# Silu of a gate and of a convolution by ScalarE's own function over whole blocks, and a re-timed order, in a fused attention, Mamba and recurrent kernel

## The reference

```python
xz = einsum('btd,de->bte', x, in_proj_w)            # 256 -> 2 x 512
x_branch, z = split(xz, 2)
xb = depthwise_conv(x_branch, conv_w, 4 taps) + conv_b
x_branch = silu(xb)                                  # "xc" in the kernel
B_t, C_t, dt = split(x_branch @ x_proj_w, [16, 16, 1])
dt = softplus(dt * dt_proj_w + dt_proj_b)
h = exp(dt * A) * h + dt * B_t * x_branch            # 16 states, scan over time
y = (sum_s h * C_t + D * x_branch) * silu(z)
return y @ c_proj_w
```

## Time and profile before

| | |
|---|---|
| median of 3 runs | 1284.66 us (1284.48 to 1288.39) |
| the profiled execution, its own time | 1291.45 us |
| span of the profile within it | 1290.1 us |
| TensorE busy | 1144.3 us (89%) |
| VectorE busy | 1172.5 us (91%) |
| ScalarE busy | 781.7 us (61%) |
| GpSimd busy | 981.8 us (76%) |
| mean granted clock | 0.968 |

### The profile page before, as it was taken

One profiled execution on the slowest core, in us unless ns is written; L12 is line 12 of the kernel. 1 busy time (PEld: TensorE's weight loads), 2 busy tenths in 40 slices (PEclk: granted clock), 3 DMA queues, 4 the chain that ended last, 5 costly groups with the idle time before them and its releaser, 6 DMA issues.

```text
span 1290.1 us, 12503 instructions
## 1 busy us (share of the span) xinstructions
PE 1144.3 (89%) x3574; PEld 640.0 (50%) x3574; DVE 1172.5 (91%) x1161; ACT 781.7 (61%) x1447; POOL 981.8 (76%) x713
## 2 busy tenths in 40 slices
PE   6767967898899989998999899998999898789896
PEld 4533523474447543673447543673447443444454
DVE  3666899999999999999999999999999999999987
ACT  2226645856667657855767657865776666645532
POOL 3213795889879897989878997989878996976852
PEclk9778988999999999999999999999999999899999
DMA  6406567775768678876769687876868676899922
GB/s 252 139 5 220 209 226 258 282 261 213 250 227 303 235 251 290 288 259 224 251 227 308 213 281 277 299 251 212 265 219 302 219 270 219 303 322 345 371 88 98
DMA packets 92309, 313.87 MB, mean 243 GB/s; under 512 B 10432, under 2 KB 15680, under 8 KB 91984
## 3 DMA queue, kind: packets, MB, share of 16 engines
q1 hardware_dynamic: 89216, 303.77, 68.1%
q10 hardware_dynamic: 3024, 9.31, 2.0%
HBM read 301.73 MB, written 11.31 MB: 243 GB/s over the span
## 4 chain that ended last, share of the span: by engine, by line
PE 40%; DVE 28%; POOL 12%; issue 9%; ACT 6%; DMA 4%; DVEq 0%; SPq 0%; POOLq 0%; ACTq 0%
DVE ps L1667 15%; PE ps L857 14%; POOL arena L1894 6%; PE ps L568 5%; DVE ps L1390 4%; PE ps L791 4%; DVE arena L1673 3%; PE ps L576 3%; DMA arena<-bc_scratch 2%; PE ps L695 2%; PE ps L703 2%; PE ps L711 2%; PE ps L718 2%; PE ps L600 1%; DVE stats_before L1271 1%
## 5 line engine op out<-in xcount | busy, mean ns | idle before, releaser
L1894 POOL TENSOR_TENSOR arena<-arena 128x1024 f32<-128x1024 f32 x255 | 600.2, 2361 | 157.3 <-PE ps L857 126.1
L1667 DVE TENSOR_TENSOR_SCAN ps<-ps,arena 128x1024 f32<-128x1024 f32 (+1 forms) x257 | 585.8, 2280 | 24.6 <-ACT ps L1236 15.8
L857 PE MATMUL ps<-arena,identF 128*128 128x512 f32 x1024 | 485.4, 605 | 47.2 <-DVE arena L1673 28.3
L1236 ACT ACTIVATE ps<-arena,negA 128x512 f32<-128x512 f32 x512 | 333.0, 683 | 87.4 <-DVE arena L1673 82.5
L857 PEld LDWEIGHTS ps<-arena,identF 128*128 128x128 f32 x1024 | 190.9, 194 | 267.6 <-issue 203.0
L1673 DVE TENSOR_TENSOR arena<-ps,arena 128x1024 f32<-128x1024 f32 x256 | 311.8, 1218 | 5.7
L872 ACT ACTIVATE arena<-arena,rnln 128x256 f32<-128x256 f32 x120 | 63.0, 589 | 50.9 <-POOL rnln L1700 37.6
L614 PE MATMUL ps<-arena,inw 128*128 128x512 f32 x128 | 62.5, 635 | 20.0 <-ACT arena L881 9.6
L1390 DVE SCALAR_TENSOR_TENSOR ps<-arena,vecs,ps 128x512 f32<-128x512 f32 x96 | 64.8, 747 | 5.9 <-ACT ps L985 5.9
L695 PE MATMUL ps<-arena,inw 128*128 128x512 f32 x128 | 61.1, 600 | 3.3 <-DVE arena L1554 3.3
L881 ACT ACTIVATE arena<-ps,modT 128x512 f32<-128x512 f32 x45 | 54.1, 1267 | 13.9 <-PE ps L454 13.5
(11 more groups left out here) (220 smaller groups left out, 1675.9 us busy)
## 6 DMA issues: line engine op xcount, KB each, us to landing
arena<-bc_scratch SPq DMA_DIRECT2D x511, 512.0 KB, 5.0
arena<-in_x SPq DMA_DIRECT2D x16, 256.0 KB, 6.7
arena<-in_x SPq DMA_DIRECT2D x8, 512.0 KB, 8.1
xr_scratch<-arena SPq DMA_DIRECT2D x6, 512.0 KB, 6.6
px_scratch<-arena SPq DMA_DIRECT2D x6, 512.0 KB, 7.0
out_x<-arena SPq DMA_DIRECT2D x5, 512.0 KB, 2.6
arena<-bc_scratch SPq DMA_DIRECT2D x9, 256.0 KB, 3.6
rowmod<-mod_scratch SPq DMA_DIRECT2D x4, 512.0 KB, 8.7
```

Source lines behind the costliest of these rows:

```text
L857: x = pe.matmul(ps[:, Y, :], identF[:], inp[:, m % RING, q, :], start=False, stop=(i == BLOCK_STEPS - 1 and q == 1), skip_group_check=True)
L1236: x = act.activation(ps[:, 2 * (m % 2) + q, :], dt[:, kd, :], ACT.Exp, scale=negA[:, kd, 2 * i + q:2 * i + q + 1])
L1667: x = dve.tensor_tensor_scan(states, states, inp[:, m % RING, q, :].rearrange("p q t -> p (q t)"), 0.0, ALU.mult, ALU.add)
L1894: x = pool.tensor_tensor(inp[:, m % RING, :, :], u[:, kd:kd + 1, :].broadcast_to([P, 2, TH]), b_at[:, m % 3, :, :], ALU.mult)
```

## The change

Both silus are computed by ScalarE's `Silu` function over larger tiles in SBUF.

- z: ScalarE copies each kd from the bank to `sz` (four copies of 128x512), which frees the bank, and then computes Silu once over all of `sz`, 128x2048, in place. The first gate of a half waits for that one instruction. `dve_z` is gone.
- convolution: VectorE's third tap writes its sum to `xc` instead of the bank; ScalarE computes Silu in place over `xc` of kd 0 and 1 and of kd 2 and 3 (two of 128x1024), both behind the last tap. `dve_silu` and the tanh are gone. TensorE's channels of kd 2 and 3 now wait for the last tap of kd 0 and 1.
- Silu and Exp are in different tables of ScalarE, as are Softplus and Exp, so ACT_TABLE_LOAD instructions stand around each new Silu. The program has 49 of them, where it had 18.
- the factors 1/2 that were folded into D, `dtw`, the projection weights and `GA1` go, with four small instructions at the start.
- `TIMES` has new numbers nearly throughout, for all five engines.

```diff
-MAMBA = ["pad", "xb_mm", "xc_init", "conv", "xc_tanh", "xc", "z_mm", "z_tanh", "z_ev", "bc_mm", "bc_sb", "softplus", "spare",
+MAMBA = ["pad", "xb_mm", "xc_init", "conv", "xc", "z_mm", "z_ev", "z_silu", "bc_mm", "bc_sb", "softplus", "spare",
...
-    "pe_after": {"c_proj": (1, 3.75), "z": (5.25, 6, 7.25, 9), "hnA_t0": 10.25, "hnA_t1": 11,
+    "pe_after": {"c_proj": (1, 3), "hnA_t0": 8.75, "hnA_t1": 9.25, "gate_x": (11.25, 12.75, 17, 17.75, 20.75, 23.75),
+        "gate_c": (11.25, 12.75, 17, 17.75, 20.75, 24.75), "px": (25, 26), "om": 26, "z": (4, 5, 6, 6.75)},
...
                 if kd >= 2:
-                    pe.wait_ge(S.xc, 4 * h + kd - 1)
+                    pe.wait_ge(S.conv, conv_done(h, kd - 2, TAPS - 2))
...
+        def act_silu(h, p):
+
+            act.wait_ge(S.conv, conv_done(h, 2 * p + 1, TAPS - 2))
+            act.activation(xc_pair(h, p), xc_pair(h, p), ACT.Silu).then_inc(S.xc, 2)
...
-                if kd % 2:
-                    for r in (kd - 1, kd):
-                        yield t + T["xc_tanh"][r]
-                        act.wait_ge(S.conv, conv_done(h, r, TAPS - 2))
-                        act.activation(xb[:, r, 0:TH], ps[:, X0 + r % 2, :], ACT.Tanh, scale=0.5).then_inc(S.xc_tanh, 1)
+            yield t + T["xc_silu"]
+            for p in range(2):
+                act_silu(h, p)
...
-                act.activation(sz[:, kd, :], ps[:, Y0, :], ACT.Tanh, scale=0.5).then_inc(S.z_tanh, 1)
+                act.activation(sz[:, kd, :], ps[:, Y0, :], ACT.Copy).then_inc(S.z_ev, 1)
...
+            yield t + TIMES["act_after"]["z_silu"]
+            act.wait_ge(S.z_ev, 4 * (g + 1) + 4)
+            act.activation(sz, sz, ACT.Silu).then_inc(S.z_silu, 1)
...
-            dve.scalar_tensor_tensor(x, xb[:, kd, tap:tap + TH], vec("conv", kd * TAPS + tap), x,
-                                     ALU.mult, ALU.add).then_inc(S.conv, 1)
-
-        def dve_silu(h, kd, bank):
-
-            dve.wait_ge(S.xc_tanh, 4 * h + kd + 1)
-            dve.scalar_tensor_tensor(xc_of(h, kd), xb[:, kd, 0:TH], 1.0, ps[:, bank, :], ALU.add, ALU.mult).then_inc(S.xc, 1)
+
+            dve.scalar_tensor_tensor(xc_of(h, kd) if tap == TAPS - 2 else x, xb[:, kd, tap:tap + TH],
+                                     vec("conv", kd * TAPS + tap), x, ALU.mult, ALU.add).then_inc(S.conv, 1)
...
-        def dve_z(h, kd):
-            dve.wait_ge(S.z_tanh, 4 * h + kd + 1)
-            dve.scalar_tensor_tensor(sz[:, kd, :], sz[:, kd, :], 1.0, ps[:, Y0, :], ALU.add, ALU.mult).then_inc(S.z_ev, 1)
...
-            dve.wait_ge(S.z_ev, 4 * g + kd + 1)
+            dve.wait_ge(S.z_silu, g + 1)
             dve.wait_ge(S.y, 2 * m + 2)
```

140 lines of the change are left out of this document (61 added, 79 removed), and 18 rows, old and new, of the table TIMES.

## The result

The changed kernel takes 1294.43 us (median of 20 runs, 1289.34 to 1299.79), the kernel before 1288.22 us over the same 20 rounds (its median of three runs was 1284.66). The ratio is 1.005, 95% interval 1.0035 to 1.0065. So it is slower by half a per cent, 6.2 us over the same rounds, where 12.2 us less was forecast (1272.5 us from 1284.66). The range was 1248 to 1294 us, and the result lies just above it. Three single executions of kernels of the experiments took 2952 to 3999 us at a granted clock of 1.00; the ratios leave them out.

What follows compares the result with a forecast made beforehand. VectorE bounds steps 16 to 23, TensorE steps 24 to 7, with a mixed stretch between. Convolution -17.9, z place +6.6, start -1.0 sum to -12.3 us: 1272.5 us from 1284.66. Own range 1264 to 1281, full range 1248 to 1294.

Steps and rivals of the forecast that it cites:

- The z place: Steps 4 to 10: gate 1.6 to 1.8 us later, one z product gone; +1.1 us per half, +6.6 over six.
- made good: TensorE's sum of step 8 starts 3.1 us later for Dx; earlier transposes and vanished waits recover 2.6 us.
- The prices on ScalarE: At z: copy 0.6 us, table load 1.28, Silu of 128x2048 1.95, between 1.9 and 2.9.
- The convolution: Steps 20 to 23: four VectorE products leave, 2.55 us per half in seven halves, -17.9 us.
- so TensorE's next piece comes forward with them: Steps 20 to 23: TensorE's channels and projection wait for VectorE's products (0.42 and 0.32 us), so they start earlier.
- what TensorE had earlier from steps 21 to 23 stays: Steps 24 to 31: TensorE is full and wins nothing more, but its projection starts sooner, so the gain stays.
- up to one step: If SyncE's earlier x load waits for the residual, B and C rows come up to 4 us late per half.
- The load's price: Each new ScalarE table load costs 1.28 us and no more; 31 loads make 39.8 us.
- the rule of the Trainium skill: A drain of about 1.38 us beside each 1283 ns load, 2.66 us per switch; 31 loads would be 82 us.
- Rival (3): Slower: ScalarE's load, Silu, load (4.5 us) at the z place delay gate and Dx; some 1295 us, chance 0.19.
- the start: First half's convolution, before the scan: four products (2.7 us) leave, one more load (1.28) comes; about -1 us.
- 2.85 us of gate wait: First half's z and the last one's: 2.7 us of products gone against this wait, about 0.

Runs made afterwards that it cites:

- spare products: Changed kernel with four 128x512 products nobody reads on TensorE, ahead of the recurrence's first transposes; ratio 0.9991 to the kernel before, 1288.38 us.
- the old order: Kernel before with the convolution's part alone (two Silu, its products gone), z and every order number as before; ratio 0.9979, 1284.72 us.

## Why the prediction was wrong, point by point

**The z place, +1.1 us per half forecast, +2.8 measured** (16.8 / 6). This is the main miss. The term failed in two ways.

First, it priced TensorE's idle time by its length and then called it made good ("2.6 of the 3.1 us are made good"). The wait for Dx grew from 1.81 us to 4.64, and behind it TensorE ran at its lower level. The spare products show the price, 8.4 us over six halves, 1.4 each. The making good was also misread: of the transposes, "two times 0.6 us", only the first four stand ahead of the wait (736.01), the others behind it (743.08). The text had no term for the clock at all, though the trace of before has it. Steps 8 to 15 of two halves of one kind in that kernel:

```profile
296.79:333.66 36.87, 31.73 (x88) 15.11 (x86) 34.07 (x27) 19.60 (x31) 34.74 (x28) 0.95 0.58 205
584.38:620.19 35.81, 29.32 (x85) 14.23 (x84) 34.07 (x28) 19.15 (x30) 34.34 (x28) 1.00 0.61 212
```

Two of its six halves stand at 0.95, which costs them 1.1 us each. All quarters of the sample had 1.00, and so it went unseen. With the clock kept up by spare products the place costs 1.4 us per half (222.5 against 214.1), near the 1.1 forecast.

Second, z was moved ahead of four products of the sums, and the sentence counted only that z comes earlier. The gate needs the sum of step 7 as well as Silu, and would wait 2.6 us for it without the loads. That sum ended at 731.42 and now ends at 736.18 less 2.55 us, by which this half as a whole is later: 2.2 us later, of which the last z ahead of it takes 1.7. The gate was forecast 1.6 to 1.8 us late and came 2.5 late (736.87 less the same 2.55 us, against 731.82), because the last z ended at 730.2 (732.74 less 2.55) and not at 729.4. Among the reasons, a sum record was priced at 0.47 us, while in a run of them one starts every 0.43. The prices on ScalarE were right: Silu 1.92 for 1.95, load 1.28; Dx was forecast 3.1 us late and came 3.7.

**The convolution, -2.55 us per half forecast.** In the old order, where it can be read alone, VectorE's stretch gets 1.9 us shorter and the half's period 0.6. The four rows add up to 2.59 us, but each product moves the next instruction by only 0.57 to 0.60 us (799.38 to 799.95 for the third), 2.35 us in all. The step that failed is "so TensorE's next piece comes forward with them", taken for the full 2.55 us, and behind it "what TensorE had earlier from steps 21 to 23 stays". What there was to gain on TensorE stood in the earlier trace rows: its waits for VectorE are 0.42 and 0.32 us, 0.74 together. Its projection came 0.9 us earlier, and of this 0.3 to 0.6 us went again in the gapless stretch behind it. The loads of the convolution cost about 0.7 us per half there, where the prediction took them at 0.

**SyncE, 0 forecast with "up to one step" in the range.** The place was named and priced at nothing, and the range of 1264 to 1281 has no term for it either. What waits is not the load of x but that of the modulation rows behind it. It cost 2.05 and 1.94 us in the middle halves. Taking it away alone gave 1.2 us over six halves, since VectorE's copy then met a GpSimd instruction.

**The load's price** was right, 1.28 us with 0.01 us behind it (734.92 after 733.63 + 1.28), and the rule of the Trainium skill ("ScalarE: Activation LUTs", section What ACT_TABLE_LOAD costs) that the prediction weighed, 2.66 us per switch, is not borne out here. Rival (3), the z place passing its full price into TensorE's chain, had the right sign and place, and its condition was met: the place costs 2.8 us, more than 2.55. But its mechanism, 4.5 us of ScalarE in full, was not what happened; of the 9.4 us that the loads cost at z, 8.4 came back with the clock. That its 1295 us is near the 1294.43 measured is luck. In the balance of the six halves: forecast 6 x (1.1 - 2.55) = -8.7, measured +7.7; the z place accounts for 10.2 of the 16.4 us between them, 8.4 of these by the clock, and the other three quarters for 6.3 (15.3 forecast, 9.0 gained), of which the two waits for the C row are 4.0 by their length. Outside these halves the profiled execution is 0.9 us shorter, where the forecast had 3.6 (the start and the seventh convolution). The "2.85 us of gate wait" that it set against the products of the first and the last half is in no row.

## What to carry to other kernels

When an engine's wait grows, ask whether TensorE's clock survives it: behind a wait of 4.6 us the lower clock cost 1.4 us per half here, and filling the wait with products nobody reads gave the time back. When a piece is moved ahead of others in an engine's list, write down what the others are now late for. An order tuned for one set of waits can be a loss for another (2.8% here), so a function and its order have to be tried together, part by part. Before work is taken off an engine as a test, look whether what stands behind it in the list can come forward at all; here it waited for VectorE, and the test said nothing.
